# An S4D filter and a gated FFN in one kernel: the complex gain as (E + 1) Q + E h, with part of it on GpSimd, and a different split of the last tile

## What is computed

```python
# x: 128 x 32 x 512 (batch, channel, position); N = 64 states per channel
dt = exp(log_dt);  A = -exp(log_A_real) + 1j * A_imag;  dtA = A * dt
Ct = (C0 + 1j * C1) * (exp(dtA) - 1) / A
K = 2 * real(einsum('hn,hnl->hl', Ct, exp(dtA * arange(512))))     # one filter of 512 taps per channel
y = causal_convolution(x, K) + x * D                                # then masked by length[batch]
y = fp8_round(y)
h = fp8_round(silu(y @ gate.T) * (y @ up.T))                        # 512 -> 1376
out = x + h @ down.T                                                # 1376 -> 512
```

## Time and profile before

| | before |
|---|---|
| median of 3 runs | 325.48 us |
| the profiled execution | 325.52 us |
| its span, first to last instruction | 323.8 us |
| PE busy | 310.2 us (96%) |
| DVE busy | 303.2 us (94%) |
| ACT busy | 206.9 us (64%) |
| POOL busy | 12.5 us (4%) |
| granted TensorE clock, mean | 1.000 |

### The profile page before, as it was taken

How to read it: one execution, slowest core, us unless ns; L and a number is a source line. 1 busy time by engine, 2 the same in 40 slices (tenths; PEclk the granted TensorE clock), 3 DMA queues, 4 the chain that set the end, 5 groups by cost and what they waited for, 6 DMA issues and landing times.

```text
span 323.8 us, 4771 instructions
## 1 busy us (share of the span) xinstructions
PE 310.2 (96%) x1569; PEld 162.9 (50%) x1595; DVE 303.2 (94%) x464; ACT 206.9 (64%) x318; POOL 12.5 (4%) x20
## 2 busy tenths in 40 slices
PE   1999999999999999999999999999999999989996
PEld 1467554545455554555455454555455454534444
DVE  6999999999999999999998999989998999989784
ACT  4858788188755777486845868376863959364540
POOL 2031000000001000010001000010001000010010
PEclk9999999999999999999999999999999999999999
DMA  6879999300002690078202780067401650051028
GB/s 201 181 181 231 268 278 383 148 1 2 0 0 28 150 343 3 1 130 279 110 0 36 165 317 1 0 121 249 150 0 16 134 243 0 0 97 34 2 31 228
DMA packets 14014, 38.38 MB, mean 119 GB/s; under 512 B 1470, under 2 KB 6558, under 8 KB 11052
## 3 DMA queue, kind: packets, MB, share of 16 engines
q1 hardware_dynamic: 8412, 26.58, 23.2%
q0 software_dynamic: 5584, 11.57, 20.6%
HBM read 33.90 MB, written 15.81 MB: 154 GB/s over the span
## 4 chain that ended last, share of the span: by engine, by line
PE 72%; DVE 19%; issue 4%; ACT 4%; DMA 1%; DVEq 0%; ACTq 0%
PE gate_ps L547 19%; PE up_ps L547 18%; PE down_ps L503 17%; PE y_ps L489 15%; DVE hv L860 3%; DVE yq L844 3%; DVE yt L833 2%; DVE hq L877 2%; DVE ht L868 2%; PE y_ps L598 1%; DVE ym L825 1%; PE down_ps L598 1%; ACT hc L381 1%; DMA prm<-in_params 1%; DVE hq L885 1%
## 5 line engine op out<-in xcount | busy, mean ns | idle before, releaser
L398 ACT ACTIVATE sil<-gate_ps,fac 128x512 f32<-128x512 f32 (+1 forms) x88 | 59.6, 680 | 67.8 <-PE gate_ps L547 66.8
L547 PE MATMUL gate_ps<-yq,wg 128*128 128x512 bf16 (+3 forms) x365 | 88.2, 363 | 2.7 <-DVE hv L860 2.4
L547 PE MATMUL up_ps<-yq,wu 128*128 128x512 bf16 (+3 forms) x367 | 88.4, 363 | 0.3
L489 PE MATMUL y_ps<-xt,toep 128*128 128x512 f32 (+1 forms) x248 | 78.1, 434 | 0.0
L503 PE MATMUL down_ps<-wd,hq 128*128 128x512 bf16 (+1 forms) x295 | 76.8, 379 | 0.7
L860 DVE SCALAR_TENSOR_TENSOR hv<-up_ps,fac,sil 128x512 f32<-128x512 f32 (+1 forms) x88 | 65.5, 744 | 8.2 <-ACT sil L398 6.6
L381 ACT ACTIVATE hc<-hv 128x1024 f32<-128x1024 f32 (+1 forms) x48 | 47.0, 980 | 20.9 <-DVE hq L877 19.8
L547 PEld LDWEIGHTS gate_ps<-yq,wg 128*128 128x128 bf16 x372 | 35.6, 100 | 43.6 <-ACT sil L398 4.0
L489 PEld LDWEIGHTS y_ps<-xt,toep 128*128 128x128 f32 x248 | 45.9, 190 | 19.9 <-issue 2.4
L868 DVE SCALAR_TENSOR_TENSOR ht<-hc,hv 128x1024 f32<-128x1024 f32 (+1 forms) x48 | 54.1, 1127 | 1.9 <-ACT hc L381 1.9
L547 PEld LDWEIGHTS up_ps<-yq,wu 128*128 128x128 bf16 x372 | 36.3, 100 | 38.3
(11 more groups left out here) (155 smaller groups left out, 118.1 us busy)
## 6 DMA issues: line engine op xcount, KB each, us to landing
xt<-in_xT SPq DMA_DIRECT2D x8, 1024.0 KB, 7.6
out<-in_x SPq DMA_DIRECT2D x7, 1024.0 KB, 5.6
out<-res POOLq DMA_DIRECT2D x7, 1024.0 KB, 7.8
toep<-kpad_scratch SPq DMA_DIRECT2D x6, 1024.0 KB, 10.0
toep<-kpad_scratch SPq DMA_DIRECT2D x8, 256.0 KB, 3.9
wd<-in_down POOLq DMA_DIRECT2D x1, 1280.0 KB, 21.3
xt<-in_x SPq DMA_DIRECT2D x1, 1024.0 KB, 7.3
out<-xt SPq DMA_DIRECT2D x3, 256.0 KB, 3.1
```

The costliest lines, as they stand in the source:

```text
L398: nc.scalar.activation(sil[b][0:w, :], gate_ps[b][0:w, :], ACT.Silu, scale=fac[0:w, S_GATE:S_GATE + 1]).then_inc(silu_done, 1)
L489: last = nc.tensor.matmul(y_ps[h % 2][:, d * P:L], toep[par][:, h, d * P:(d + 1) * P], xt[par][:, h, 0:L - d * P], start=(d == 0), stop=(d ...
L547: mm = nc.tensor.matmul(ps[b][0:w, cols], wt[:, k, c * P:c * P + w], yq[par][:, version, k, cols], start=(k == 0), stop=(k == LB - 1))
```

## The change

The complex factor is computed by another formula. With exp(dtA) = (1 + E)(cos + i sin), E = exp(x) - 1 and h = 2 C conj(A) / |A|^2 (signs folded into a doubled, negated C), it is (E + 1) Q + E h, where Q = h (cos - 1 + i sin). Of it, |A|^2 and C times conj(A) are finished by five `tensor_tensor` on GpSimd, behind `decay_ready`, with new semaphores `norm_ready` and `gain_ready` for which VectorE waits. The D terms of group 0 are full matmuls of 64 columns (one row holding D and zeros, loaded with the identity) ahead of its taps, so that the last tap completes the sum. Warm-ups: one small, the taps of group 0, one small, five large. VectorE's masks 0 and 1 move behind the turns of group 1 and the product of group 2, masks 2 and 3 behind the coefficients of group 1, and the damping of group 1 follows the turns of group 2. The last tile is split 384 and 128.

```diff
...
 K_GROUPS = [slice(0, FIRST), slice(FIRST, 6), slice(6, JC)]
-WARM = (2, 14)
+WARM = (1, 1, 5)
 EARLY, MIDDLE = 2 * P, 5 * P
...
 dec = inside(hq[0], 0, JC, M)
-one_by_one, by_step = inside(hq[0], JC * M, 1, P), inside(hq[0], JC * M + P, LATE, M)[0:LATE]
-decay_t = inside(hq[0], JC * M + P + LATE * M, 1, P)[0:LATE]
+unit_tile = inside(hq[0], JC * M, 1, P + FIRST * KB)
+one_by_one = unit_tile[:, :, 0:P]
+dsk_first = unit_tile[:, 0, P:].rearrange("p (j b) -> p j b", b=KB)
+by_step = inside(hq[0], JC * M + P + FIRST * KB, LATE, M)[0:LATE]
+decay_t = inside(hq[0], JC * M + P + FIRST * KB + LATE * M, 1, P)[0:LATE]
 gu, gv = inside(hq[1], 0, JC, 2, KA), inside(hq[1], 2 * JC * KA, JC, 2, KA)
...
     sp.dma_start(bass.AP(kpad, 0, [[ROW, C], [1, PADK]]), zrow[:, 0:PADK]).then_inc(zeros_in, 16)
-    sp.dma_start(one_by_one[:, 0], unit).then_inc(unit_in, 16)
+    sp.dma_start(unit_tile[:, 0], unit).then_inc(unit_in, 16)
     sp.dma_start(by_step, stepped).then_inc(unit_in, 16)
...
     pool.dma_start(wu[:, :, 0:EARLY], wu_d[:, :, 0:EARLY]).then_inc(up_in, 16)
+
+    def s(i, n=1):
+        return sm[:, i:i + n, :]
+
+    pool.wait_ge(decay_ready, 1)
+    nc.gpsimd.tensor_tensor(s(27), s(9), s(9), ALU.mult).then_inc(gain_chain, 1)
+    nc.gpsimd.tensor_tensor(s(31, 2), s(37, 2), s(9).broadcast_to([P, 2, JC]), ALU.mult).then_inc(gain_chain, 1)
+    pool.wait_ge(gain_chain, 1)
+    nc.gpsimd.tensor_tensor(s(27), s(27), s(28), ALU.add).then_inc(norm_ready, 1)
+    pool.wait_ge(gain_chain, 2)
+    nc.gpsimd.tensor_tensor(s(33), s(31), s(30), ALU.subtract)
+    nc.gpsimd.tensor_tensor(s(34), s(29), s(32), ALU.add).then_inc(gain_ready, 1)
     pool.wait_ge(toep_first[HB - 1], 16)
...
+    def unit_terms(i):
+
+        js = K_GROUPS[i]
+        for half in range(2):
+            row = slice(N * half, N * half + 1)
+            unit_row = cst[row, UNIT:UNIT + KA]
+            if i == 0:
+                nc.tensor.matmul(k_in_bank(0, half), unit_row, dsk_first[row], start=True, stop=False)
+            else:
+                nc.tensor.matmul(k_in_bank(i, half)[:, :, 0], unit_row, dsk[row, js],
+                                 start=False, stop=True).then_inc(k_ready, 1)
+
     def k_of(i):
...
                 for half, rows in enumerate(halves):
-                    nc.tensor.matmul(k_in_bank(i, half)[:, j - js.start], gk[rows, j, t],
-                                     wave[rows, j, t, 0:KB], start=(j == js.start and t == 0), stop=False)
-        for half in range(2):
-            row = slice(N * half, N * half + 1)
-            nc.tensor.matmul(k_in_bank(i, half)[:, :, 0], cst[row, UNIT:UNIT + KA], dsk[row, js],
-                             start=False, stop=True).then_inc(k_ready, 1)
+                    last = i == 0 and j == js.stop - 1 and t == 1
+                    mm = nc.tensor.matmul(k_in_bank(i, half)[:, j - js.start], gk[rows, j, t],
+                                          wave[rows, j, t, 0:KB], start=(i > 0 and j == js.start and t == 0),
+                                          stop=last)
+                    if last:
+                        mm.then_inc(k_ready, 1)
+        if i:
+            unit_terms(i)
+
+    def warm_small(count):
+        for n in range(count):
+            nc.tensor.matmul(y_ps[n % 2][:, 0:6 * JC + CONSTS], prm[:, 0:P], prm[:], start=True, stop=True)
...
                          stop=True).then_inc(dec_arg_ready, 1)
-    for n in range(WARM[0]):
-        nc.tensor.matmul(y_ps[n % 2][:, 0:6 * JC + CONSTS], prm[:, 0:P], prm[:], start=True, stop=True)
+    unit_terms(0)
+    warm_small(WARM[0])
     k_of(0)
+    warm_small(WARM[1])
     pe.wait_ge(gate_in, 16)
-    warm(WARM[1])
+    warm(WARM[2])
     k_of(1)
...
                             (2, range(6), full), (0, range(8, CH), full), (1, range(8, CH), full),
-                            (2, range(6, CH), full), (3, range(CH), slice(0, L // 2)),
-                            (3, range(CH), slice(L // 2, L))):
+                            (2, range(6, CH), full), (3, range(CH), slice(0, 3 * P)),
+                            (3, range(CH), slice(3 * P, L))):
         for k in chunks:
...
     thetas, kt, r = s(15, 3), s(0, 3), s(10, 3)
-    x, kx, rx, qx, two_x = s(19), s(20), s(21), s(22), s(23)
-    expm1, norm, half = s(25), s(27), s(28)
-    c_ai, c_ar, g = s(29, 2), s(31, 2), s(33, 2)
-    gre, gim = s(33), s(34)
-    sr, si, g_sr, g_si = s(35), s(36), s(29, 2), s(31, 2)
+    x, kx, rx, qx, two_x, rt_x = s(19), s(20), s(21), s(22), s(23), s(24)
+    expm1, norm, ai2 = s(25), s(27), s(28)
+    c_ai, c2, h = s(29, 2), s(37, 2), s(33, 2)
+    h_cos, h_sin, turned, cos1 = s(29, 2), s(31, 2), s(35, 2), s(26)
...
     e = did(v.tensor_scalar(ex, ex, -87.0, 88.0, ALU.max, ALU.min))
-    v.tensor_tensor(c_ai, cc, both(ai), ALU.mult)
+    v.tensor_scalar(c2, cc, -2.0, None, ALU.mult)
     after(e)
     e = did(v.tensor_scalar(ek, ex, LOG2E, MAGIC, ALU.mult, ALU.add))
-    v.scalar_tensor_tensor(half, ai, 0.5, ai, ALU.mult, ALU.mult)
+    v.tensor_tensor(ai2, ai, ai, ALU.mult)
     after(e)
     e = did(v.tensor_scalar(ek, ek, MAGIC, None, ALU.subtract))
+    v.tensor_tensor(c_ai, c2, both(ai), ALU.mult)
     after(e)
...
     b = did(v.scalar_tensor_tensor(qx, qx, 1.0 / math.factorial(5), rx, ALU.add, ALU.mult))
-    c = did(v.scalar_tensor_tensor(norm, ar, 0.5, ar, ALU.mult, ALU.mult))
+    v.tensor_scalar(two_x.bitcast(I32), kx, 127.0, 2.0 ** 23, ALU.add, ALU.mult)
+    dve.wait_ge(norm_ready, 1)
+    c = did(v.reciprocal(norm, norm))
     after(b)
     b = did(v.scalar_tensor_tensor(qx, qx, 1.0 / math.factorial(4), rx, ALU.add, ALU.mult))
-    v.tensor_tensor(c_ar, cc, both(ar), ALU.mult)
     after(b)
     b = did(v.scalar_tensor_tensor(qx, qx, 1.0 / math.factorial(3), rx, ALU.add, ALU.mult))
-    c = did(v.tensor_tensor(norm, norm, half, ALU.add))
+    v.tensor_tensor(rt_x, rx, two_x, ALU.mult)
+    dve.wait_ge(gain_ready, 1)
+    after(c)
+    c = did(v.tensor_tensor(h, h, both(norm), ALU.mult))
     after(b)
     b = did(v.scalar_tensor_tensor(qx, qx, 1.0 / math.factorial(2), rx, ALU.add, ALU.mult))
-    v.tensor_scalar(two_x.bitcast(I32), kx, 127.0, 2.0 ** 23, ALU.add, ALU.mult)
-    after(b)
-    b = did(v.scalar_tensor_tensor(qx, qx, 1.0, rx, ALU.add, ALU.mult))
-    c = did(v.reciprocal(norm, norm))
-    after(b)
-    b = did(v.tensor_tensor(qx, qx, two_x, ALU.mult))
-    v.tensor_tensor(gre, s(30), s(31), ALU.subtract)
-    c = did(v.tensor_tensor(gim, s(29), s(32), ALU.add))
+    dve.wait_ge(sines_ready, 1)
+    a = did(v.scalar_tensor_tensor(cos1, s(SIN_HALF), -2.0, s(SIN_HALF), ALU.mult, ALU.mult))
+    after(b)
+    b = did(v.scalar_tensor_tensor(qx, qx, 1.0, rt_x, ALU.add, ALU.mult))
     after(c)
+    c = did(v.tensor_tensor(h_sin, h, both(s(SIN)), ALU.mult))
+    after(a)
+    a = did(v.tensor_tensor(h_cos, h, both(cos1), ALU.mult))
+    after(b)
     b = did(v.scalar_tensor_tensor(expm1, two_x, -1.0, qx, ALU.add, ALU.add))
-    dve.wait_ge(sines_ready, 1)
-    a = did(v.scalar_tensor_tensor(sr, s(SIN_HALF), -2.0, s(SIN_HALF), ALU.mult, ALU.mult))
-    c = did(v.tensor_tensor(g, g, both(norm), ALU.mult))
     after(a)
-    a = did(v.scalar_tensor_tensor(sr, expm1, 1.0, sr, ALU.add, ALU.mult))
-    b = did(v.scalar_tensor_tensor(si, expm1, 1.0, s(SIN), ALU.add, ALU.mult))
+    v.tensor_tensor(s(35), s(29), s(32), ALU.subtract)
+    a = did(v.tensor_tensor(s(36), s(31), s(30), ALU.add))
     damped = [decayed(0)]
+    after(b)
     after(a)
-    a = did(v.tensor_tensor(sr, sr, expm1, ALU.add))
-    after(b)
-    b = did(v.tensor_tensor(g_si, g, both(si), ALU.mult))
+    v.scalar_tensor_tensor(h_cos, both(expm1), 1.0, turned, ALU.add, ALU.mult)
+    a = did(v.tensor_tensor(h_sin, both(expm1), h, ALU.mult))
     after(a)
-    a = did(v.tensor_tensor(g_sr, g, both(sr), ALU.mult))
-    after(a)
-    v.tensor_tensor(s(38), s(29), s(32), ALU.add)
-    a = did(v.tensor_tensor(s(39), s(31), s(30), ALU.subtract))
+    a = did(v.tensor_tensor(s(38, 2), h_cos, h_sin, ALU.add))
...
         js = K_GROUPS[i]
-        w = damped[0] if i == 0 else decayed(i)
+        w = damped[i]
         after(a)
...
         v.tensor_copy(rows_of_k(0, half), k_in_bank(0, half)).then_inc(k_first, 1)
-    after(last)
-    v.tensor_scalar(mask[:, 0, :], lenf[:], cst[:, LEN0:LEN0 + 1], None, ALU.is_gt)
     after(w)
...
     w = did(v.tensor_tensor(in_steps(turns[:, js]), tau_by_j(js), steps(js), ALU.mult))
+    after(last)
+    v.tensor_scalar(mask[:, 0, :], lenf[:], cst[:, LEN0:LEN0 + 1], None, ALU.is_gt)
+    after(w)
+    w = did(v.tensor_scalar(whole[:, js], turns[:, js], MAGIC, MAGIC, ALU.add, ALU.subtract))
     v.tensor_scalar(mask[:, 1, :], lenf[:], cst[:, LEN0 + 1:LEN0 + 2], None, ALU.is_gt)
     after(w)
-    w = did(v.tensor_scalar(whole[:, js], turns[:, js], MAGIC, MAGIC, ALU.add, ALU.subtract))
+    v.tensor_tensor(turns[:, js], turns[:, js], whole[:, js], ALU.subtract).then_inc(turns_ready, 1)
+    damped.append(decayed(1))
+    g_of(1)
```

(18 more changed lines are left out.)

## The result

The changed kernel takes 326.83 us in the median of 22 runs (324.84 to 328.23), the kernel before 325.57 (325.29 to 326.22, 22 runs) beside it: a ratio of 1.0033, 95% interval 1.0020 to 1.0047, so slower by a third of a per cent. (The ratios here leave out executions over 1.5% above the fastest of their kernel and need not be the quotient of the medians beside them.) The width is as telling as the median. Of the 22 executions, 6 took 324.84 to 325.45 us, 2 about 326.1, 7 took 326.60 to 327.49 and 7 took 327.79 to 328.23. The profiled one is of the last group (328.23, span 326.5), 2.71 us above the profiled one of before.

A forecast was written before the change was run, and what follows sets the result against it. The loop was taken as bound by TensorE, the start by VectorE's dependent chain. From 325.52 us, 0.62 for the front and 0.13 for the end were subtracted, giving 324.77, say 324.8 us; range 324.4 to 326.0.

The forecast's parts named there:

- What bounds the kernel: Loop bound by TensorE and untouched, so it moves as a whole with the front; start bound by VectorE's dependent chain.
- Complex product: VectorE's chain at the start: 19 instructions instead of 24, L788's place at 10.48 instead of 10.97, 0.49 us earlier.
- D terms: Group 0, ahead of the taps: first copy waits only for the last tap, 11.88 us, 0.13 us more won.
- VectorE's other path: Masks and damping at the front: VectorE free at 18.88 instead of 19.66, 0.78 us earlier.
- GpSimd: Five products at the start: 0.2 us each, done at 7.1, hidden; each may last 0.54 before VectorE waits.
- Rival (a): GpSimd and VectorE hinder each other at 6 to 7.5 us: up to 0.95 us, likelier 325.2 us; chance 0.17.
- Rival (b): GpSimd's products are long: at 0.93 us each VectorE stalls 1.96 us, time 326.7 us; chance 0.06.
- The path to the first taps: Store 12.25, Toeplitz load 13.74, first taps 17.15 instead of 17.77; collision with early weights 0 to 0.3 us, taken as 0.
- rival (d): Edits work, but the store meets the weights and the last tile's 192 KB land last: 325.4 us; chance 0.09.
- Warm-ups: TensorE ahead of the first convolution: five large instead of 14, over at 14.85; fewer needed to use the gain, thinnest place.
- rival (c): First taps still at 1.2 GHz: first channel 4.9 us instead of 2.44, 327.4 us; partly slow, 326.0; chance 0.13.
- The end: Last tile split 384 and 128: last residual 0.35 instead of 0.48 us; worth -0.13 to +0.3 us, 0.13 won taken.

The follow-up runs named there:

- e13: Repeat of e9: the changed kernel with 10 large warm-ups and the up weights' load moved behind the first Toeplitz load; 325.25 us, ratio 0.9989.
- e8: e5 with the D terms of group 0 behind its taps again, as narrow as before; 326.24 us, ratio 1.0015.
- e5: The changed kernel with 10 large warm-ups and the up weights' load moved behind the last of the first Toeplitz loads; 325.31 us, ratio 0.9974.
- e7: e5 with the five products of GpSimd back on VectorE; 326.55 us, ratio 1.0032.
- e9: The changed kernel with 10 large warm-ups and the up weights' load moved behind the first Toeplitz load; 324.71 us, ratio 0.9987.
- e1: The changed kernel with 10 large warm-ups instead of 5, nothing else; 325.26 us, ratio 0.9984.
- e4: The kernel before with only the last tile's split changed to 384 and 128 columns; 325.68 us, ratio 0.9988.
- e2: The kernel before with 5 large warm-ups instead of 14, nothing else of the change; 327.35 us, ratio 1.0049.
- e10: The changed kernel with 10 large warm-ups and the up weights' load issued once the first copies of k are made; 326.14 us, ratio 1.0012.
- e11: e10 with 8 large warm-ups instead of 10; 327.65 us, ratio 1.0047.

## Why the prediction was wrong, by its own steps

**What bounds the kernel: right.** The rest kept its length (262.37 and 262.33 us from the second block's start), and what the front lost was carried to the end. In e13 the loop took back most of what the front gave.

**Complex product: right.** L788's place was put at 10.48 and is at 10.49. The extra head instructions cost nothing that shows.

**D terms: right.** First copy 11.88, store 12.25, both as computed; e8 gives 0.11 for a step put at 0.13.

**VectorE's other path: right.** Coefficients of group 1 complete near 15.81 (taps start 15.85), last damping 16.13 (16.11), VectorE free at 18.88 (18.53 + 0.32 = 18.85).

**GpSimd: right.** 0.21 to 0.26 us each against 0.2, over at 7.16 against 7.1, and no wait for `norm` or `h` shows. My estimate from the Trainium skill's figure (GPSIMD Engine Reference, Performance versus the Vector engine), 0.10 to 0.13 us, is half of what was measured at these sizes. Rival (a), 0.17, is out: VectorE's pace beside the products changed by 0.02 us over 1.4. The Trainium skill (SBUF — State Buffer, Who interferes with whom) says that a VectorE instruction with two SBUF inputs contends with a GpSimd instruction that reads SBUF. The trace doesn't contradict it: one such instruction, beside the last product, takes 0.21 us in e5 where its like takes 0.17 in e7. But it prices next to nothing here, and no run shows larger work. Rival (b) is out too.

**The path to the first taps: mis-sized.** The collision of store and weights was charged 0, with 0.3 as bound. It is 0.43 after (1.92 against 1.49 from store to Toeplitz issue), 0.61 with ten warm-ups (2.10), 0 once the load is moved (1.48). The transfers' landings say the same: the 8 KB store lands after 1.4 us in before and in e9, 1.8 after, 2.0 in e1. That the up weights do it is shown by e5 and e9, which differ from e1 only in their place. I had seen the DMA share of 0.89 just behind its new place, and argued it away by "its data move about a microsecond behind its issue". A microsecond behind 12.25 the up load was still under way: issued at 4.93, it landed 8.9 us later, near 13.8. By what the two hold each other up isn't shown; the DMA share is already down to 0.23 between 13.0 and 13.5. The load itself took 0.10 more to the first taps (3.51 against 3.41). With the first taps at 17.68 instead of 17.15, 0.53 of the 0.62 us is gone at once. This is half of rival (d).

**Warm-ups: the step that failed.** I had read that after's stretch of work without a gap is no longer than the one that came ahead of the change of pace, called it the thinnest place, and still took the fast clock for granted, giving rival (c) 0.13. The reading itself hung on the one trace of before, in which the pace changed at about 15 us; in others it changed up to 2.6 us later, and in the changed kernel's it had not when the five ended at 14.99. By their times and clocks 14 of 22 executions were slow at the first taps; one of them is seen in a trace. Its price was right in kind: the whole first channel at 1.2 GHz was put at 4.9 us and took 4.63. In the profiled execution the slow pace lasted beyond it: from 17.68 to about 23.3 us TensorE did half its work, which loses 2.8 us. 324.77 + 0.53 + 2.8 = 328.1, where 328.23 was measured; the last two terms are read from the same execution, so the sum only shows that nothing large is missing. The median of 326.83 is a mixture, 2 us more than the forecast. That the same kernel shows different numbers of slow matmuls from run to run is what the Trainium skill says as well (TensorE: Matmul & The Clock Gate, The HAM clock gate); the traces agree, with the last slow weight load anywhere from 13.7 to 17.6 us, and a forecast from one profiled execution of before could not have given their shares, but it had to give this case far more than 0.13.

**The end: right in sign, small.** Residuals of 384 and 128 columns take 0.62 and 0.35 us (0.35 forecast); 192 KB landed in 1.9 us, better than the 2.2 to 2.5 assumed, the last 64 KB in 1.7. From the end of TensorE's work to the end of the span it is 0.1 us shorter (2.53 against 2.63); e4's times can't resolve it.

**Open.** Whether the number of warm-ups or the length of the gap behind them decides can't be said in general: e2 and the change alter both, e10 and e11 alter only the number and differ. Why the version with products on VectorE loses 0.7 to 1.2 us where its front loses 0.33 to 0.4 is not settled either, nor why e13 and e5 stay 0.5 us above the forecast in the median.
